# Cross attention: the transposes of the row maxima and their reduction, one step later

## The reference

```python
def _gqa(q, k, v):
    scale = 1.0 / np.sqrt(q.shape[-1])
    scores = jnp.einsum('bsghd,btgd->bghst', q, k) * scale
    p = jax.nn.softmax(scores, axis=-1)
    return jnp.einsum('bghst,btgd->bsghd', p, v)
...
qx = _ln(qx, qxln_w, qxln_b)
kvx = jnp.einsum('bsi,oi->bso', cond, w_kv_x)
kx, vx = jnp.split(kvx, 2, axis=-1)
kx = _ln(kx.reshape(b, sc, g, d), kxln_w, kxln_b)
vx = vx.reshape(b, sc, g, d)
xout = _gqa(qx, kx, vx).reshape(b, s, nh * d)
```

## Time and profile before

| | us |
|---|---|
| median of 3 runs | 2570.34 |
| lowest, highest | 2569.04, 2573.16 |
| profiled execution, its own time | 2567.38 |
| its span | 2565.4 |
| busy in the span: PE / PEld / DVE / ACT / POOL | 2334.2 / 2035.8 / 2072.5 / 1087.9 / 972.2 |

### The profile page before, as it was taken

One profiled execution on the slowest core, in us unless ns is written; L12 is line 12 of the kernel. 1 busy time (PEld: TensorE's weight loads), 2 busy tenths in 40 slices (PEclk: granted clock), 3 DMA queues, 4 the chain that ended last, 5 costly groups with the idle time before them and its releaser, 6 DMA issues. The chain is left out here.

```text
span 2565.4 us, 38211 instructions
## 1 busy us (share of the span) xinstructions
PE 2334.2 (91%) x12603; PEld 2035.8 (79%) x12603; DVE 2072.5 (81%) x3952; ACT 1087.9 (42%) x1849; POOL 972.2 (38%) x640
## 2 busy tenths in 40 slices
PE   7999999999985788769999999999999999986797
PEld 6777777879973666658888888888888888876797
DVE  8999987877758878848988988889889888981487
ACT  1000001118855666615454545454545554554332
POOL 5565100200012444425555554555555545570000
PEclk9999999999986888879999999999999999997899
DMA  9667623527624011032222211222222112106211
GB/s 388 258 268 274 250 90 144 190 75 252 223 94 137 37 44 41 38 133 80 68 74 83 72 63 55 83 83 67 74 83 71 57 62 83 60 4 162 56 54 40
DMA packets 143384, 286.66 MB, mean 112 GB/s; under 512 B 26033, under 2 KB 114178, under 8 KB 139202
## 3 DMA queue, kind: packets, MB, share of 16 engines
q1 hardware_dynamic: 137266, 265.40, 30.0%
q0 software_dynamic: 6032, 20.20, 2.1%
HBM read 203.91 MB, written 81.66 MB: 111 GB/s over the span
## 5 line engine op out<-in xcount | busy, mean ns | idle before, releaser
L1691 POOL TENSOR_TENSOR s_acc<-s_acc,s_sx 125x896 f32<-125x896 f32 x128 | 322.1, 2516 | 223.1 <-ACT s_sx L1755 220.6
L1755 ACT ACTIVATE s_sx<-s_sx 125x896 f32<-125x896 f32 x192 | 183.7, 957 | 448.9 <-DVE s_sx L1903 448.9
L572 DVE BATCH_NORM_STATS2 s_st<-ps 125x6 f32<-125x128 f32 x1536 | 318.6, 281 | 54.6 <-PE ps L444 48.5
L1890 DVE TENSOR_TENSOR s_sx<-ps,keep_krs 125x896 f32<-125x896 f32 x192 | 208.5, 1086 | 125.7 <-PE ps L1801 124.5
L1845 PE MATMUL ps<-s_p_hi,s_cn_hi 125*128 125x448 f32 x768 | 301.0, 392 | 4.0 <-DVE s_p_lo L1909 3.5
L1801 PE MATMUL ps<-s_qc_hi,s_ct_hi 128*125 128x448 f32 x768 | 289.8, 377 | 1.3 <-issue 1.3
L1845 PE MATMUL ps<-s_p_lo,s_cn_hi 125*128 125x448 f32 x768 | 282.8, 368 | 0.0
L1845 PE MATMUL ps<-s_p_hi,s_cn_lo 125*128 125x448 f32 x768 | 282.7, 368 | 0.0
L1801 PE MATMUL ps<-s_qc_lo,s_ct_hi 128*125 128x448 f32 x768 | 281.9, 367 | 0.0
L1801 PE MATMUL ps<-s_qc_hi,s_ct_lo 128*125 128x448 f32 x768 | 281.6, 367 | 0.0
L1909 DVE TENSOR_TENSOR s_p_lo<-s_sx,s_p_hi 125x896 fp32r<-125x896 f32 x192 | 268.6, 1399 | 1.6 <-ACT s_p_hi L1760 1.5
(11 more groups left out here) (378 smaller groups left out, 5648.6 us busy)
## 6 DMA issues: line engine op xcount, KB each, us to landing
l_ahead<-in_ctxt SPq DMA_DIRECT2D x16, 1500.0 KB, 8.3
s_ct_hi<-ct_hi SPq DMA_DIRECT2D x48, 500.0 KB, 4.2
s_ct_lo<-ct_lo SPq DMA_DIRECT2D x48, 500.0 KB, 4.9
s_cn_raw<-in_ctx SPq DMA_DIRECT2D x48, 500.0 KB
l_raw<-in_ctxt SPq DMA_DIRECT2D x15, 1500.0 KB, 10.2
l_raw<-in_w SPq DMA_DIRECT2D x16, 1024.0 KB, 5.4
ct_hi<-l_hi SPq DMA_DIRECT2D x8, 1500.0 KB, 11.9
ct_lo<-l_lo SPq DMA_DIRECT2D x8, 1500.0 KB, 16.1
```

What stands on the lines that cost most here:

```text
L572: ins = dve.bn_stats(st[:, G * t + g, :], kx[0:TT, t % NB, g // 4, DH * (g % 4):DH * (g % 4) + DH])
L1691: pool.tensor_tensor(a, a, p[:, PR * w.pt:PR * w.pt + PR, :], ALU.add).then_inc(s["acc_ready"], 1)
L1755: act.activation(p, p, ACT.Exp).then_inc(s["exp_ready"], 1)
L1890: dve.tensor_tensor(by_group(sx[w.h][:, tiles, :]), by_group(sc[st % 2]), krs_b[:, tiles, HG * w.h:HG * w.h + HG].unsqueeze(3).to_broadcas ...
```

## The change

The four transposes and the reduction move from step 0 to step 1 of the next unit. On TensorE they now stand behind the scores of step 1, ahead of its probabilities; on VectorE behind the scaling L1890 of step 1, ahead of the subtraction. The waits are the same ones. No instruction is added or removed, and ScalarE, GpSimd and SyncE keep their lists.

```diff
@@ tensor
                         mm.then_inc(s["sc_ready"], 1)
+                    if w.i == 1 and w.one_back:
+                        pe.wait_ge(s["mx_ready"], w.u)
+                        if not (static(b) and w.u < 3):
+                            pe.wait_ge(s["v_read"], w.u - 2)
+                        for j in range(HG):
+                            mm = pe.transpose(misc[0:PAIR, TT * j:TT * j + TT], mx[:, PAIR * j:PAIR * j + PAIR], keep.ident[0:TT, 0:TT])
+                        mm.then_inc(s["mt_ready"], 1)
                     if w.i == 2 and w.one_back:
                         pe.wait_ge(s["diag_ready"], w.u)
...
                         mm.then_inc(s["pv_ready"], 1)
-                    if w.i == 0 and w.one_back:
-                        pe.wait_ge(s["mx_ready"], w.u)
-                        if not (static(b) and w.u < 3):
-                            pe.wait_ge(s["v_read"], w.u - 2)
-                        for j in range(HG):
-                            mm = pe.transpose(misc[0:PAIR, TT * j:TT * j + TT], mx[:, PAIR * j:PAIR * j + PAIR], keep.ident[0:TT, 0:TT])
-                        mm.then_inc(s["mt_ready"], 1)
@@ vector
                                           krs_b[:, tiles, HG * w.h:HG * w.h + HG].unsqueeze(3).to_broadcast([TT, PR, HG, PAIR]), ALU.mult).then_inc(s["sc_read"], 1)
+                    if w.i == 1 and w.one_back:
+                        dve.wait_ge(s["mt_ready"], w.u)
+                        if not (static(b) and w.u < 2):
+                            dve.wait_ge(s["diag_ready"], w.u - 1)
+                        dve.tensor_reduce(m4[:, :], misc[0:PAIR, 0:HG * TT].rearrange("p (g n) -> p g n", g=HG), AX.X, ALU.max).then_inc(s["mt_read"], 1)
...
-                    if w.i == 0 and w.one_back:
-                        dve.wait_ge(s["mt_ready"], w.u)
-                        if not (static(b) and w.u < 2):
-                            dve.wait_ge(s["diag_ready"], w.u - 1)
-                        dve.tensor_reduce(m4[:, :], misc[0:PAIR, 0:HG * TT].rearrange("p (g n) -> p g n", g=HG), AX.X, ALU.max).then_inc(s["mt_read"], 1)
```

## The result

The changed kernel took 2575.43 us (median of 17 runs, 2571.11 to 2579.26) and the kernel before, on the same chip, 2571.52 us (17 runs, 2568.96 to 2573.56): ratio 1.0015, 95% interval 1.0008 to 1.0022. That is 3.9 us slower (2.1 to 5.7): the interval leaves out zero, and the difference is smaller than the 0.2% (5.1 us) that the prediction took as the least that can be told from no change. The forecast was 2573.0 us and +2.7; the time is inside its range.

A forecast was written before the change was run, and what follows sets the result against it. TensorE was taken to set the pace in cross attention. Even units 0, odd units +2.7 us and ends 0, added to the 2570.34 us median, gave 2573.0 us; own range 2570 to 2575, full range 2567 to 2579.

The forecast's parts named there:

- Even units, gain 0: Units with h=0: the wait for the maxima becomes a 1.9 to 2.2 us wait for `p_lo`; gain 15 x 0.
- Reduction against fold: Even units: the later reduction ends at 1986.2, the query fold comes at 1987.19; 1.0 us to spare, cost 0.
- Odd units, +0.19 a pair: Units with h=1: reduction +0.59, earlier scores -0.40, so +0.19 us reaches the sums; 14 x 0.19 = +2.7 us.
- The link through GpSimd: Odd units: L1935's end, not the exponential (+0.33 us), decides when GpSimd's addition ends; it passes +0.19 us on.
- Rival A: TensorE's even-unit gap of 1.6 to 2.0 us closes: whole, 27 us faster, 2543; chance 0.11 (0.04 whole).
- Rival B: Odd units pay the reduction in full on the way to `qc_lo`: up to 8.3 us slower, 2578.6; chance 0.23.
- The level: Whole kernel: median of the runs shown, 2570.34 us, plus 2.7 gives 2573.0 us.

The follow-up runs named there:

- e1: Transposes and reduction moved in even units (h=0) only, odd units as in the kernel before: 2573.52 us, ratio 1.0008 to the kernel before.
- e4: Changed kernel with probability matmuls reading `p_hi` in place of `p_lo` and not waiting for `p_lo` (part of the computation left out): 2563.63 us, ratio 0.9968.
- e5: Transposes and reduction moved in odd units (h=1) only, even units as in the kernel before: 2576.67 us in a single run.
- e11: e10 plus GpSimd's `cn_lo` of the first block waiting for the unit's second `qc_lo`; everything computed: 2542.82 us, ratio 0.9891.
- e9: Kernel before, GpSimd's third-block `cn_lo` computed for only 2 of 256 columns except in the first batch row: 2547.96 us, ratio 0.9907.
- e10: Kernel before plus one wait: GpSimd's third-block `cn_lo` waits for the joined maximum; everything computed: 2552.16 us, ratio 0.9921.
- e8: e7 with `p_lo` first only inside the loop over batch rows: 2558.87 us, ratio 0.9948.
- e7: Kernel before, but in even units transposes behind step 1's scores and `p_lo` first in step 0, reduction still ending step 0: 2562.57 us, ratio 0.9959.
- e2: Kernel before with only VectorE's reduction moved behind step 1's scaling, transposes staying in step 0: 2595.53 us, ratio 1.0097.

## Why the prediction was right

- **Even units, gain 0: right, shown.** The step was that `p_lo` ends at the same moment as the old wait. The matmul stands 0.05 us behind `p_lo`; the new wait is 1.72 us on the matmul and 1.96 on the weight load (forecast 1.9 to 2.2, a little high for the first: it counted the weight load's 0.24 us in both). e1 shows that the move there gives no time, e4 that it would give some if `p_lo` weren't needed.
- **Reduction against fold: right.** 1.0 us to spare, as worked out. At the start, where no probabilities stand between, the fold waits for it once, 1.3 us; the stretch to the first sums is 0.05 us longer.
- **Odd units, +0.19 a pair: the path right, the size within 0.03.** Whole pairs give 73.642 - 73.450 = 0.19, and 14 of them 2.7 us, but the odd units' share is 0.17 and the even units, forecast at 0, give the other 0.03: that the sum meets 0.19 to the second digit is luck. The single steps are all a little smaller than forecast (L1935 +0.16 for 0.19, the exponential +0.30 for 0.33, the scores read 0.42 earlier for 0.40, the wait at the sums 0.74 for 0.77). e5 shows the cost in the odd units alone.
- **The link through GpSimd: right.** The addition ends 1.99 us behind L1935, before and after, though its exponential comes 0.14 us later against L1935: L1935 decides. The Trainium skill (SBUF — State Buffer, Who interferes with whom) says that a VectorE instruction with two SBUF inputs contends with a GpSimd instruction that reads SBUF. By that rule the addition can be held by L1935, and `p_lo` and L1940 by `cn_lo`. The trace agrees: `p_lo` ends 0.94 us behind `cn_lo` (1961.97 and 1961.03), the same `p_lo` takes 1.08 us once e11 takes `cn_lo` away from it, and L1940 takes 0.62 once e9 and e10 do. The addition's own part (2.85 us beside L1935, 2.12 for one of the same size alone) is read from rows; no run took L1935 away from it.
- **Rival A: wrong as forecast, and a part of it could be had.** It needed `p_lo` earlier; e8, which gives it that, gains 13 us, half of A's 27. By the rows of e7 the rest goes to collisions with GpSimd. The Trainium skill (Perfetto Trace Analysis, Optimization Strategy) says to find the gap and the semaphore that blocks and to make that dependency start sooner or complete faster. e10 does the second, the maximum takes 0.62 us instead of 2.68, and it is worth 19 us, where moving the waiting work was worth nothing.
- **Rival B: its path is real, its price too low.** Paid in full, the reduction costs 23 us (medians) and not 8.3. The delay is the forecast one (0.58 a pair in the five pairs at full clock); nine falls of the clock at some 1.5 us each are the larger part (e2). The prediction had no term for the clock.
- **The level.** The forecast said +2.7; the medians say +3.9 (2.1 to 5.7). The profile finds 2.7 of it in the pairs; the rest is within the interval. The time is 2.4 us over the forecast 2573.0: 1.2 of them are the kernel before, whose median over 17 runs is 2571.52 and not the 2570.34 of the three shown.

## What to carry to other kernels

Before moving work into a gap, look for the second wait that ends at the same moment: here a distance of 0.06 us between the next needed result and its consumer told that the gap would only change its name. When the late result comes from an instruction at several times its usual duration (2.68 us against 0.62), move what it collides with, not what waits for it: one added wait on an engine with slack was worth 19 us here, two 28. Count a pause on TensorE by its clock too, not by its length alone.

## What was not expected of the hardware

- A pause of 1.17 us ahead of the sums (1 column each) dropped the granted clock in nine pairs of 14: 0.58 over the next 4.1 us, about 1.5 us lost. The other five odd units have the same pause and keep 1.00. Pauses of 1.6 to 2.0 us ahead of full matmuls in the even units (and of 0.58 and 0.74 ahead of the same sums) show no such loss: the clock there is 1.00. What tells the cases apart wasn't tried.
- Beside `cn_lo` on GpSimd the 0.62 us maximum took 2.68, the 1.08 us `p_lo` 2.22, 2.37 and 3.28, while `cn_lo` itself took 2.4 to 3.2. In these cases the delayed VectorE instruction ends a fixed time behind GpSimd's (0.94 or 0.95 us for `p_lo`, 0.48 for the maximum), nearly its whole undisturbed duration.
- Because of the clock, delays don't add up evenly: +0.16 us of wait at the odd units' sums went with +0.19 a pair, +0.59 with +1.56.
